# Rest probabilities: high and low parts of two pairs in one operand, and centring that waits only for the moments

## What is computed

```python
# x: (32, 256, 256); context: (32, 77, 512); 16 heads of 64
x = x + tanh(g_xattn) * xattn(layernorm(x), context)
x = x + tanh(g_ffn)   * ffn(layernorm(x))

def xattn(x, context):
    q = heads(x @ Wq) * 64 ** -0.5
    k, v = heads(context @ Wkv)                 # 77 keys, and one learned "null" key and value: 78
    attn = softmax(q @ k.T)                     # (32, 16, 256, 78)
    out = merge(attn @ v) @ Wout                # "PV", then the output projection
    return (out - mean(out)) * rsqrt(var(out) + 1e-6) * ln_scale + ln_bias
```

## Time and profile before

| What | us |
|---|---|
| Median of three runs | 2132.0 |
| Profiled execution | 2131.79 |
| its span, first to last instruction | 2130.0 |
| TensorE busy, of the span | 2009.3 |
| VectorE busy | 1697.5 |
| ScalarE busy | 1359.0 |
| GpSimd busy | 1205.8 |

### The profile page before, as it was taken

How to read it: one execution, slowest core, us unless ns; L and a number is a source line. 1 busy time by engine, 2 the same in 40 slices (tenths; PEclk the granted TensorE clock), 3 DMA queues, 4 the chain that set the end, 5 groups by cost and what they waited for, 6 DMA issues and landing times.

```text
span 2130.0 us, 42507 instructions
## 1 busy us (share of the span) xinstructions
PE 2009.3 (94%) x13730; PEld 1836.1 (86%) x13730; DVE 1697.5 (80%) x4060; ACT 1359.0 (64%) x3966; POOL 1205.8 (57%) x1322
## 2 busy tenths in 40 slices
PE   7999688999999999999996899999999999999994
PEld 7888578999999999999996788888888888888884
DVE  5544257888888888888887766668999999999996
ACT  2211356777777777777773257777777777777771
POOL 0001203777777777777777500007777777777775
PEclk9999899999999999999998899999999999999997
DMA  8664388987777777777787999999999999999997
GB/s 274 214 194 165 124 258 295 305 256 240 244 242 236 241 247 241 240 242 247 239 275 235 314 333 285 287 285 386 402 403 401 397 392 389 402 393 393 396 360 276
DMA packets 400531, 625.60 MB, mean 294 GB/s; under 512 B 170935, under 2 KB 275096, under 8 KB 397848
## 3 DMA queue, kind: packets, MB, share of 16 engines
q1 hardware_dynamic: 351160, 488.60, 67.7%
q0 software_dynamic: 49152, 134.28, 17.5%
HBM read 315.08 MB, written 307.63 MB: 292 GB/s over the span
## 4 chain that ended last, share of the span: by engine, by line
PE 30%; DVE 22%; DMA 14%; POOL 11%; issue 8%; ACT 3%; SPq 1%; DVEq 0%; POOLq 0%; ACTq 0%
DMA w_raw<-in_experts 12%; POOL pages_dram L842 6%; DVE parts L1811 4%; PE ring L140 4%; PE ring L142 3%; PE ring L141 3%; PE xps L1910 2%; DVE minus_max L1022 2%; PE sim L1284 2%; POOL of_key L849 2%; DVE hid_l L1868 2%; DVE w_l L1785 2%; DVE outT_l L1169 2%; POOL x L871 2%; PE yps L140 2%
## 5 line engine op out<-in xcount | busy, mean ns | idle before, releaser
L1702 POOL DMA_INDIRECT parts<-results_dram,kept_index x512 | 518.7, 1013 | 381.3 <-DMA results_dram<-y 220.2
L842 POOL DMA_INDIRECT pages_dram<-rows,kept_index x512 | 509.5, 995 | 167.6 <-issue 139.2
L921 ACT ACTIVATE exps<-sim,minus_max 128x78 f32<-128x78 f32 x1024 | 320.9, 366 | 38.6 <-DVE minus_max L1022 38.6
L921 ACT ACTIVATION_READ_ACCUMULATOR exps<-sim,minus_max 128x1 f32 x1024 | 252.3, 247 | 0.0
L1723 ACT ACTIVATE w_h<-w_raw 128x768 fp32r<-128x768 f32 x159 | 134.0, 843 | 146.8 <-DMA w_raw<-in_experts 146.8
L1811 DVE SCALAR_TENSOR_TENSOR parts<-parts,kept_weight 128x256 f32<-128x256 f32 x448 | 213.5, 476 | 3.2 <-DMA parts<-dense_dram 2.0
L140 PE MATMUL yps<-w_h,hid_h 128*128 128x256 f32 x636 | 181.9, 286 | 4.1 <-DVE hid_l L1868 3.2
L1785 DVE TENSOR_TENSOR w_l<-w_raw,w_h 128x768 fp32r<-128x768 f32 x159 | 151.9, 956 | 38.1 <-ACT w_h L1723 37.9
L1910 PE MATMUL xps<-ident,xin 128*128 128x128 f32 x1272 | 173.4, 276 | 7.9 <-issue 4.9
L142 PE MATMUL yps<-w_l,hid_h 128*128 128x256 f32 x636 | 178.3, 280 | 0.0
L141 PE MATMUL yps<-w_h,hid_l 128*128 128x256 f32 x636 | 177.8, 280 | 0.0
(11 more groups left out here) (258 smaller groups left out, 6643.1 us busy)
## 6 DMA issues: line engine op xcount, KB each, us to landing
xin<-pages_dram SPq DMA_DIRECT2D x159, 512.0 KB, 10.8
results_dram<-y SPq DMA_DIRECT2D x159, 512.0 KB, 9.6
w_raw<-in_experts SPq DMA_DIRECT2D x159, 385.0 KB, 9.3
pages_dram<-blank SPq DMA_DIRECT2D x108, 512.0 KB
pages_dram<-blank SPq DMA_DIRECT2D x12, 1536.0 KB
values_dram<-values SPq DMA_DIRECT2D x16, 1024.0 KB
v_main<-values_dram SPq DMA_DIRECT2D x64, 256.0 KB
keys_dram<-keys SPq DMA_DIRECT2D x16, 616.0 KB, 4.2
```

Of the source, the lines that this page charges most:

```text
L842: pool.indirect_dma_start(dram["pages"], bass.IndirectOffsetOnAxis(ap=kept_index[:, at:at + 1].bitcast(U32), axis=0), buffer(batch)[:, k / ...
L921: last = act.activation(exps[u % 2][:, h, :], scores(u)[:, h // 4, h % 4, :], ACT.Exp, bias=minus_max[u][:, h:h + 1], accum_out=row_sum[u] ...
L1702: pool.indirect_dma_start(parts[slot(batch, t)][:, k, :], None, done, bass.IndirectOffsetOnAxis(ap=kept_index[:, at:at + 1].bitcast(U32), ...
```

## The change

1. The rest probabilities get 128 columns instead of 112: four strips of 32, one for each pair of a half, of which 28 are used. The unused columns are zeroed once by POOL (`pads_zeroed`).
2. Their transposes `T1b` and `T3b` fill 128 partitions: pairs 0 and 1 in the lower 64, pairs 2 and 3 in the upper 64. `high` copies each half to `pR[:, side]` in its own 64 partitions (two ACT instructions of 64 partitions instead of one of 112); `low` writes the low part of the same half to the other 64 partitions of the same side (two DVE instructions instead of one).
3. `v_rest` holds each head's values twice, in the strip of the high part and in that of the low part. So a pair's rest takes two matmuls (high values and low values against `pR[:, side]`) instead of three. Each head's values and each null row are loaded by two DMAs instead of one.
4. `centre` waits for `aggregated[1]` (the moments, which DVE itself makes) instead of `rstd_done[1]`; `residual` waits for `rstd_done[1]`.

```diff
-    probs = [sb(f"probs{i}", [P, PAIRS * J]) for i in range(2)]
-    pT = [sb(f"pT_{s}", [P, HP + 1, N], F32R) for s in "hl"]
+    probs = [sb(f"probs{i}", [P, PAIRS * DH + P]) for i in range(2)]
+    pT = [sb(f"pT_{s}", [P, HP, N], F32R) for s in "hl"]
+    pR = sb("pR", [P, 2, N], F32R)
...
+    def rest_rows(head):
+
+        first = head // 2 % 2 * STRIP + head % 2 * REST
+        return [slice(first + side, first + side + REST) for side in (0, HALF)]
...
-                sp.dma_start(rest[head * REST:(head + 1) * REST - 1, :, head // 2, col:col + DH].bitcast(F32),
-                             by_head[DH:M, :, head, :]).then_inc(values_loaded[batch % 2], 16)
+                for strip in rest_rows(head):
+                    sp.dma_start(rest[strip.start:strip.stop - 1, :, head // 2, col:col + DH].bitcast(F32),
+                                 by_head[DH:M, :, head, :]).then_inc(values_loaded[batch % 2], 16)
...
+            if name in ("T1b", "T3b"):
+                for side in range(2):
+                    strip = slice(side * HALF, (side + 1) * HALF)
+                    last = act.activation(pR[strip, side, :], bank(name, b)[strip, 0:N], ACT.Copy)
+                return signal(last)
...
         def centre(b):
-            dve.wait_ge(rstd_done[1], b)
+            dve.wait_ge(aggregated[1], b)
...
             dve.wait_ge(applied[1], b)
+            dve.wait_ge(rstd_done[1], b)
...
+            if name in ("T1b", "T3b"):
+                for side in range(2):
+                    strip, other = slice(side * HALF, (side + 1) * HALF), slice((1 - side) * HALF, (2 - side) * HALF)
+                    last = dve.tensor_tensor(pR[other, side, :], bank(name, b)[strip, 0:N], pR[strip, side, :].bitcast(F32), ALU.subtract)
+                return signal(last)
...
-                    last = split_product(pe, ps[:, i * N:(i + 1) * N], [rest_values(b, part, half, pair) for part in range(2)],
-                                         [t[0:PAIRS * REST, HP, :] for t in pT], start=False, stop=i == 1)
+                    for part in range(2):
+                        last = pe.matmul(ps[:, i * N:(i + 1) * N], rest_values(b, part, half, pair), pR[:, pair // 2, :],
+                                         start=False, stop=i == 1 and part == 1)
```

More of the change, by code:

```diff
@@ L101 @@
 REST = J - DH
+STRIP = P // HP
+HALF = P // 2
 BUFFERS = 3
@@ L595, in attention_phase @@
     gate_ready, rows_ready = sem("gate_ready"), sem("rows_ready")
+    pads_zeroed = sem("pads_zeroed")
     x_loaded, res_loaded = sem("x_loaded"), sem("res_loaded")
@@ L629, in rest_values @@
     def rest_values(batch, part, half, pair):
-        return v_rest[batch % 2][0:PAIRS * REST, part, half, pair, :]
+        return v_rest[batch % 2][:, part, half, pair, :]
+    def rest_rows(head):
+        first = head // 2 % 2 * STRIP + head % 2 * REST
+        return [slice(first + side, first + side + REST) for side in (0, HALF)]
     def buffer(batch):
@@ L653, in destination @@
             return by_two, [t[:, :, :] for t in (xnT if name == "X" else x2T)]
-        if name in ("T1b", "T3b"):
-            return ps[0:PAIRS * REST, 0:N], [t[0:PAIRS * REST, HP, :] for t in pT]
         if name[0] == "T":
@@ L757, in step @@
                     for head in range(PAIRS):
-                        sp.dma_start(rest[(head + 1) * REST - 1:(head + 1) * REST, :, head // 2, head % 2 * DH:(head % 2 + 1) * DH].bitcast(F32),
-                                     null_rows[:, :, :, :].rearrange("p s f d -> p (s f) d").bitcast(F32)).then_inc(null_placed, 16)
+                        for strip in rest_rows(head):
+                            sp.dma_start(rest[strip.stop - 1:strip.stop, :, head // 2, head % 2 * DH:(head % 2 + 1) * DH].bitcast(F32),
+                                         null_rows[:, :, :, :].rearrange("p s f d -> p (s f) d").bitcast(F32)).then_inc(null_placed, 16)
             fill_pages(b, 1)
@@ L810, in prepare @@
             last.then_inc(zeroed, 1)
+            for p in probs:
+                last = pool.memset(p[:, PAIRS * DH:], 0.0)
+            last.then_inc(pads_zeroed, 1)
             pool.memset(blank[:, :, :], 0.0).then_inc(blank_made, 1)
@@ L1032, in normalise @@
                 dve.wait_ge(ring_full, nth(RING, "T1b" if before_u < 2 else "T3b", before_b))
+            if n == 0:
+                dve.wait_ge(pads_zeroed, 1)
             e, inv = exps[u % 2], row_inv[u][:, :].unsqueeze(2)
             main = probs[u % 2][:, 0:PAIRS * DH].rearrange("p (h j) -> p h j", j=DH)
-            rest = probs[u % 2][:, PAIRS * DH:PAIRS * J].rearrange("p (h j) -> p h j", j=REST)
+            rest = probs[u % 2][:, PAIRS * DH:].rearrange("p (q w) -> p q w", w=STRIP)[:, :, 0:2 * REST].rearrange(
+                "p q (a j) -> p q a j", a=2)
             dve.tensor_tensor(main, e[:, :, 0:DH], inv.broadcast_to([P, PAIRS, DH]), ALU.mult)
-            dve.tensor_tensor(rest, e[:, :, DH:J], inv.broadcast_to([P, PAIRS, REST]), ALU.mult).then_inc(probs_ready, 1)
+            dve.tensor_tensor(rest, e[:, :, DH:J].rearrange("p (q a) j -> p q a j", a=2),
+                              inv.broadcast_to([P, PAIRS, REST]).rearrange("p (q a) j -> p q a j", a=2), ALU.mult).then_inc(probs_ready, 1)
         def statistics(i, src, batch):
@@ L1329, in output @@
                 for tt in range(TT):
-                    last = pe.transpose(ps[0:PAIRS * REST, tt * P:(tt + 1) * P], probs[tt][:, PAIRS * DH:PAIRS * J], ident[:, :])
+                    last = pe.transpose(ps[:, tt * P:(tt + 1) * P], probs[tt][:, PAIRS * DH:], ident[:, :])
             elif name[0] == "T":
@@ L1343, in output @@
                 half = int(name[2])
[L1344 removed]
+                pe.wait_ge(values_loaded[par], 16 * (2 + 2 * PAIRS) * (h + 1))
                 if b == 0:
[L1346 removed]
+                    pe.wait_ge(null_placed, 64 * PAIRS)
                 pairs = [2 * "ab".index(name[3]) + i for i in range(2)]
```

## The result

The changed kernel takes 2222.0 us against 2133.0 for the kernel before in the same comparison: a ratio of 1.0424, 95% interval 1.0408 to 1.0440. That is 89 us slower. The direction was forecast, but the size was three times the 29 us forecast, and the time lies 47 us above the upper end of the range.

The account below looks back on a forecast made before the run. SP's issue time was taken to pace the first batches, with TensorE, VectorE and POOL all near the full batch's length. 2131.8 + 38 (start) - 9 (25 full batches at -0.35) = 2161 us, range 2136 to 2175.

Parts of the forecast that it names:

- the first batches are paced by SP's issues: Start of attention: added DMAs delay keys; batch 1 loses 24 us, batches 2 and 3 lose 6 and 5.
- the last term: Start of attention, batches 4 to 6: SP's slack grows, 3 us added, between 0 and 13.
- In a full batch the eight issues are hidden: Full batch, SP's loads: keys land at 672.4, next scores come at 675.5, so added issues cost nothing.
- If it is gone, every us beyond is paid 25 times: Full batch: the 3 us margin between keys landing and next scores; once used up, the excess recurs 25 times.
- The sum for a full batch, -0.35: Full batch, both halves: 0.35 us saved, between -1.23 and +0.2; over 25 batches -9 us.
- TensorE's 0.96 us saved: Full batch: eight fewer matmuls of 0.12 us each, half before R and half in PV1.
- The first half: Full batch up to R: centring's 0.69 gain against T1b's split pieces and waits; taken as 0.
- (c): Rival at VectorE's and ScalarE's pieces: partition switches cost more, a batch grows by 0.2, 2175 us; chance 0.11.
- the four losses of 0.11: VectorE's low-part pieces of T1b and T3b: each switch of partition half loses 0.11 us, two per half batch.
- (a): Rival at SP: extra issues fit into its own waits, start costs 24, 31 batches gain 0.35, 2145 us; chance 0.13.
- (d): Rival at the start: batch 1 doesn't wait for keys, only late null rows cost some 15, 2136 us; chance 0.06.
- (b): Rival at T1b and T3b: pieces hide, POOL's floor gives -1.23 a batch, 2139 or 2118 us; chance 0.08.

Follow-up runs that it names:

- merged: Changed kernel, but one DMA loads two heads' values or places both their null rows, so as many DMAs as before the change: 2128.9 us.
- the run with other banks: The merged kernel with PV0a and PV0b, and T3a and Q2, changing PSUM banks: 2124.0 us.
- the run with the sides kept: The merged kernel, both low-part pieces reading the lower 64 partitions and writing the upper 64, leaving out part of the product: 2117.7 us.
- four spare: The kernel before with four more loads of 13x4x64 a batch that nobody reads, and no additional null rows: 2150.3 us.
- spread: Changed kernel, all DMAs kept, a batch's 16 v_rest loads placed by fours behind v_main, kT, x_res and the third fill: 2153.6 us.
- spare loads of 13 KB: The kernel before with eight more loads a batch and 16 more null rows that nobody reads, 13x4x64 per load: 2214.6 us.
- those of 1.6 KB: The kernel before with eight unread loads a batch and 16 unread null rows added, each load cut to 13x4x8: 2218.4 us.

## Why the prediction was right or wrong

**Right: the first batches are paced by SP's issues.** Batch 1 was forecast 24 us late and was 22.6; batches 2 and 3 lose 7.5 and 6.4 more, forecast 6 and 5. The null rows delayed the first batch's PV (idle for 13.9 us), inside that sum, as said. Mis-sized was the last term, 3 us for batches 4 to 6: they lost 10.1, within the 0 to 13 given. Together 46.5 instead of 38.

**Wrong: "In a full batch the eight issues are hidden".** This step failed, and with it some 49 us: -9 was forecast, +40 came. It followed one load, `kT`, from a `v_main` that it let start when it started before, with every other issue as long as before. The sum over SP's list was never made. From the rows of before it would have been 16.8 us of issues a batch and 7.8 more, 24.6 of 26.9, so little slack that the order of SP's waits had to be asked for. And the issues measured were those behind SP's pauses; without the pauses they grew by 3.1 us, to 27.9, and a full batch took 28.4 us. "If it is gone, every us beyond is paid 25 times" was the right consequence, but no rival carried it: the step got no chance and no price of its own, and the range ended at 2175.

**The sum for a full batch, -0.35**, measured without SP's part: -0.12 (merged). Inside the bounds, but the steps behind it were only partly right. Centring gave 0.29 alone instead of 0.69. TensorE's 0.96 us saved went nowhere: in the merged kernel VectorE waits for hardly anything but ScalarE's pieces (27.7 us in 46 waits from 480 to 1150 us) and sets the batch; of this the first part of the prediction had only said that what one engine gains the others may not follow. The first half was put at 0; there `PV0a`'s bank was missed, for its main products wait for `T1b`'s low part too (0.59 us in one batch), but the run with other banks shows that this wait only stands in place of another.

**The rivals.** (c) had the mechanism right, the pieces 0.43 us apart: the run with the sides kept puts it at 0.39 us a batch, near the four losses of 0.11 that the prediction had named, though two of the four stand at `z` and `outT_l` and not right behind the pieces. This hold is what the Trainium skill's rule on start quadrants (VectorE: DVE Perf Modes, Two Vector instructions with no wait between them) says, and the trace agrees with 0.86 us a pair against 0.75. The batch of +0.2 that (c) gave didn't come: -0.12 was measured. The Trainium skill's rule on two partition halves (DMA: Bandwidth & Descriptors, Rules for kernel authors), counted by bytes, was rightly not used: with twice the bytes and half the DMAs the loss was gone. (a) and (d) went the other way: SP had no waits to absorb the issues, and the keys were what batch 1 waited for: its scores follow the end of `kT`'s issue by 5.7 us in the changed kernel (306.86 to 312.60), by 5.8 before. (b) didn't come: POOL still waits 1.2 us a batch in the merged kernel.

Two readings were too simple, though neither entered the sum: POOL waits in a second place as well, for `weight` (7.0 us in 23 batches), and a DMA doesn't hold SP for 0.78 us "however small it is": a null row of 1 KB takes 0.57.

## What to carry to other kernels

Sum up the issuing queue's list over one period before adding DMAs to it, and count each at the length it has with no pause ahead of it; here four more a batch were free and eight cost 1.5 us each time. Where a queue is nearly full, merge transfers or spread the small ones over its list before counting bytes. And before an instruction is split in two, see whether it lies on a ring of waits through several engines: the products with their pieces cost 0.79 us a batch as long as `z` waited for POOL (27.69 against 26.90), and 0.17 when it didn't (26.78 against 26.61).

## What the runs showed of the hardware

A DMA's issue time hardly depends on its size: 782 ns for 13 partitions with 1.6 or 13 KB, 786 with 26 KB, 567 for one row of 1 KB, but 373 for `x_in`, 128 partitions with 256 KB. What sets it between these shapes no run here shows. The large ones grow when SP doesn't pause ahead of them: `x_in` takes 0.37 us in each of the 19 issues behind a pause in the 540 us of the kernels before, merged, four spare and spread, and 0.88 on average in the changed kernel. What the small loads carry doesn't make it: `x_in` takes 0.86 with spare loads of 13 KB and 0.77 with those of 1.6 KB.

On VectorE a piece from the other 64 partitions starts 0.01 us after the end of the piece before it (0.43 from start to start), and one from the same 64 partitions 0.08 before that end (0.34).
